# A decoder layer with attention and eight experts: sums of four steps in five quarters of batch two, and another passage from the attention loop to the experts, with a half-begun first expert

## The reference

```python
x = layernorm(x + linear_attention(x))             # 16 heads of 32, elu(q) + 1, elu(k) + 1
x = layernorm(x + cross_attention(x, ctx))         # 16 heads of 32, softmax over 2048 rows of context
x = layernorm(x + experts(x))

def experts(xf):                                   # 2048 tokens, 8 experts, two for each token
    probs = softmax(xf @ router_w + router_b)
    topk_p, topk_i = top_k(probs, 2)               # weights divided by their sum
    rank = place of the assignment among those of its expert, in order of the token
    keep = rank < 640                              # capacity: ceil(1.25 * 4096 / 8)
    h = gelu(buf[e] @ w1[e] + b1[e])               # 640 x 512 by 512 x 1024
    eo = h @ w2[e] + b2[e]                         # 640 x 1024 by 1024 x 512
    out[token] += eo[slot] * weight
```

## Time and profile before

| | us |
|---|---|
| median of 3 runs (1951.0 to 1957.52) | 1952.97 |
| the profiled execution's own time | 1955.99 |
| its span in the profile | 1954.2 |
| its mean granted PE clock | 0.982 of full speed |
| PE busy | 1886.4 (97%) |
| DVE busy | 1254.8 (64%) |
| ACT busy | 888.0 (45%) |
| POOL busy | 822.1 (42%) |

### The profile page before, as it was taken

One profiled execution on the slowest core, in us unless ns is written; L12 is line 12 of the kernel. 1 busy time (PEld: TensorE's weight loads), 2 busy tenths in 40 slices (PEclk: granted clock), 3 DMA queues, 4 the chain that ended last, 5 costly groups with the idle time before them and its releaser, 6 DMA issues.

```text
span 1954.2 us, 26706 instructions
## 1 busy us (share of the span) xinstructions
PE 1886.4 (97%) x10016; PEld 1281.6 (66%) x10016; DVE 1254.8 (64%) x2391; ACT 888.0 (45%) x1595; POOL 822.1 (42%) x740
## 2 busy tenths in 40 slices
PE   8999999989999999999999999999969999999996
PEld 6887677777655555555445545544439998899995
DVE  5675573257778788888678778777653444344457
ACT  3312322222566666666456456546724433344431
POOL 3002201100388788888567657665011223222132
PEclk9999999999999999999999999999978999999998
DMA  7003524573667476757434424421234444434453
GB/s 275 22 1 114 189 87 165 193 208 124 172 132 178 101 182 134 170 120 156 98 103 104 109 59 131 109 65 62 82 111 138 135 125 119 128 99 125 135 140 113
DMA packets 123777, 244.87 MB, mean 125 GB/s; under 512 B 11232, under 2 KB 29424, under 8 KB 119600
## 3 DMA queue, kind: packets, MB, share of 16 engines
q1 hardware_dynamic: 108608, 185.46, 32.0%
q0 software_dynamic: 13952, 55.61, 13.9%
q10 hardware_dynamic: 1088, 2.10, 0.3%
HBM read 148.46 MB, written 62.42 MB: 108 GB/s over the span
## 4 chain that ended last, share of the span: by engine, by line
PE 82%; DVE 13%; DMA 2%; issue 1%; ACT 1%; SPq 1%; POOL 1%; POOLq 0%; DVEq 0%; ACTq 0%
PE banks L1167 34%; PE banks L1440 12%; PE banks L1347 11%; PE banks L1317 10%; PE banks L1336 8%; DVE max L1638 8%; PE banks L1368 4%; PE banks L1173 2%; DMA k_parts<-out_lo 1%; DMA k_half<-in_xwk_t 0%; PE banks L1249 0%; DMA raw<-in_wk_t 0%; DVE stats_y L1869 0%; DVE den_c L1657 0%; POOL x_nat L2148 0%
## 5 line engine op out<-in xcount | busy, mean ns | idle before, releaser
L1638 DVE TENSOR_REDUCE max<-banks 128x1 f32<-128x512 f32 x1024 | 627.1, 680 | 144.3 <-PE banks L1317 143.4
L2137 POOL TENSOR_TENSOR probs<-probs,probs 128x512 f32<-128x512 f32 x464 | 583.0, 1291 | 249.0 <-PE banks L1347 249.0
L2017 ACT ACTIVATE probs<-banks 128x512 f32<-128x512 f32 x1024 | 520.2, 607 | 260.7 <-PE banks L1336 260.1
L1317 PE MATMUL banks<-k_stack,q_stack 98*128 98x512 f32 x1024 | 428.3, 425 | 4.0 <-DVE max L1638 2.7
L1336 PE MATMUL banks<-q_stack,k_stack 98*128 98x512 f32 x1024 | 377.1, 398 | 2.6 <-ACT probs L2017 2.6
L1317 PEld LDWEIGHTS banks<-k_stack,q_stack 98*128 98x128 f32 x1024 | 192.2, 188 | 194.5 <-DVE max L1638 106.2
L1347 PE MATMUL banks<-probs,v_grp 128*32 128x512 f32 x2048 | 251.7, 604 | 0.0
L1336 PEld LDWEIGHTS banks<-q_stack,k_stack 98*128 98x128 f32 x1024 | 191.7, 188 | 62.3 <-ACT probs L2017 17.8
L2184 POOL DMA_INDIRECT y_rows<-eo,tok x35 | 71.4, 2040 | 170.3 <-DVE eo L1839 116.1
L1826 DVE TENSOR_TENSOR hid_lo<-hid,hid_hi 128x640 fp32r<-128x640 f32 x64 | 52.8, 825 | 139.0 <-ACT hid_hi L2082 139.0
L1167 PE MATMUL banks<-w_hi,hid_hi 128*128 128x512 f32 x320 | 129.6, 405 | 2.3 <-DVE eo L1849 2.2
(11 more groups left out here) (263 smaller groups left out, 2806.7 us busy)
## 6 DMA issues: line engine op xcount, KB each, us to landing
k_stack<-k_parts SPq DMA_DIRECT2D x144, 256.0 KB, 5.3
w_raw<-in_L_ffn_w SPq DMA_DIRECT2D x16, 2048.0 KB, 8.4
probs<-probs POOLq DMA_DIRECT2D x31, 1024.0 KB, 10.1
q_stack<-q_parts SPq DMA_DIRECT2D x48, 256.0 KB
v_grp<-v_rows SPq DMA_DIRECT2D x48, 256.0 KB, 3.3
raw<-in_ctx_t SPq DMA_DIRECT2D x8, 1024.0 KB, 7.1
k_parts<-out_hi SPq DMA_DIRECT2D x32, 256.0 KB, 2.5
k_parts<-out_lo SPq DMA_DIRECT2D x32, 256.0 KB, 2.9
```

The lines of the kernel that those rows point to most:

```text
L1317: nc.tensor.matmul(out, queries_of(t)[:, j, tile_of(k)], keys_of(t)[0:STK + SHIFT, j, mc * HALF:(mc + 1) * HALF], start=True, stop=True) \
L1638: V.reduce_max(max4[:, tiles_of(t), :, :][:, k, j, mc:mc + 1], bank(bank_of["max", t, mc, k, j]), AX.X) \
L2017: S.activation(probs_of(t, s)[:, j, :], bank(bank_of["score", t, s, j]), ACT.Exp, scale=SCALE) \
L2137: G.tensor_tensor(a[:, j, :], a[:, j, :], b[:, j, :], ALU.add).then_inc(pair_added.sem, 1)
```

## The change

1. Five quarters of batch two, (turn, quarter) = (8,0), (8,1), (10,1), (13,0) and (13,1), go by fours as well: five `add_four` transfers more, five den units less. `pending` is kept sorted by due block, and a turn's den bank is begun by whichever unit comes first.
2. The third quarter of turn 7 has its den unit due one block sooner.
3. In the first three halves log_parts is no longer put into the bank by an identity product and copied back by ACT: DVE adds bank and log_parts.
4. A step WITH_PE beside one WITHOUT_PE is now taken only in turn 15.
5. In the last half y_nat goes into only two banks by an identity (tiles 0 and 1); DVE adds it to the banks of tiles 2 and 3, which now come first. log_parts goes in behind the rows.
6. In the last half's ranks the running sum comes from three more products with ones on PE, not from four small DVE operations. The copy that carries `before` on is left out there too.
7. `tokens` has two DVE operations for four.
8. The first 320 columns of the first expert's `up` f = 0 and f = 1 are multiplied by themselves (`up_first`), before and behind the last transposition (which touches only columns 512 to 639).

A few semaphores are shared or split otherwise. The core of the diff (semaphores, emptied banks and the engines' tables of stages left out):

```diff
+LAST_BEFORE_PLAIN = {(2 * NG - 1, 2)}
+
+LATER_FOURS = {(8, 0), (8, 1), (10, 1), (13, 0), (13, 1)}
...
+BY_VECTOR, BY_TENSOR = (2, 3), (0, 1)
...
-            return t * MT + s < B * NG * MT - FOUR
+            return t * MT + s < B * NG * MT - FOUR or (t, s // FOUR) in LATER_FOURS
...
-            begin_parts(b, h)
-            do("parts", b, h)
+            do("parts", b, h, ring=next_s_bank)
...
+            pending.sort(key=lambda due: due[0])
             while pending and pending[0][0] <= until:
                 _, t, s = pending.pop(0)
-                if s == (3 if by_fours(t, 0) else 1):
+                if t not in den_begun:
                     take_bank(("den", t), DEN)
+                    den_begun[t] = s
                 do("den", t, s)
                 if s == MT - 1:
                     do("copy_den", t)
-                    divisions.extend((t, q) for q in range(PIECES))
+                    tiles = BY_VECTOR + BY_TENSOR if t == LAST else range(HT)
+                    divisions.extend((t, k * SHARE + i) for k in tiles for i in range(SHARE))
                     divisions_from[0] = clock
...
-                if not busy or turn >= LAST - 2:
+                if not busy or turn == LAST:
...
-                        pending.append((clock + 4, turn, s + 1))
+                        pending.append((clock + (3 if (turn, s // FOUR) in LAST_BEFORE_PLAIN else 4), turn, s + 1))
...
         for k in range(HT):
             take_bank(("rows", b, h, k, LATE), next_s_bank.next())
+        for k in BY_TENSOR:
             do("rows_first", b, h, k)
-        begin_parts(b, h)
         loop_end = (scored, num_summed, den_summed, exp_done, num_copied, den_copied, pair_added, last_pair_added,
...
-        for k in range(HT):
+        for k in BY_VECTOR + BY_TENSOR:
             do("rows", b, h, k, LATE)
+        begin_parts(b, h)
...
+        for i in range(NS - 1):
             turn_xe(0, i)
             gather(1, i)
+        take_bank(("up", 0, 0), up_ring.next())
+        do("up_first", 0, 0)
+        turn_xe(0, NS - 1)
+        gather(1, NS - 1)
+        take_bank(("up", 0, 1), up_ring.next())
+        do("up_first", 0, 1)
...
+                    for k in range(HT - 1):
+                        accumulate(out[:, (k + 1) * E:HT * E],
+                                   [(ones[:, :], ms[:, k:k + 1, :].to_broadcast([P, HT - 1 - k, E]))], start=False,
+                                   stop=False)
+                    accumulate(out[:, 0:HT * E], [(ones[:, :], before[:, 0:1, :].to_broadcast([P, HT, E]))],
+                               start=False).then_inc(ranks_summed.sem, 1)
...
+                begun = e == 0 and f < 2
+                if not begun:
+                    free_bank("up", e, f)
...
+                up_products(e, f, (1,) if begun else (0, 1)).then_inc(up_summed.sem, 1)
...
+                    if k in BY_VECTOR:
+                        step.settle(V.tensor_tensor(row, got, row, ALU.add))
+                    done = V.bn_stats(stats4[:, k, :], row if k in BY_VECTOR else got)
...
+                    V.tensor_tensor(log_parts[:, :], bank(bank_of["parts", b, h]), log_parts[:, :], ALU.add) \
+                        .then_inc(parts_copied.sem, 1)
...
-                step.settle(V.tensor_tensor(tok_f[:, :], tok_f[:, :], table[:, 0, :], ALU.add))
-                step.settle(V.tensor_scalar(tok_f[:, :], tok_f[:, :], float(NTOK), None, ALU.add))
-                V.tensor_copy(tok[:, :], tok_f[:, :]).then_inc(tok_ready.sem, 1)
+                V.scalar_tensor_tensor(tok[:, :], tok_f[:, :], float(NTOK), table[:, 0, :], ALU.add, ALU.add) \
+                    .then_inc(tok_ready.sem, 1)
```

More of the change, by code:

```diff
@@ L518, in emptied @@
         def emptied(unit):
-            if unit[0] == "rows" and unit[-1] == LATE:
+            if unit[0] == "rows" and unit[-1] == LATE and unit[3] in BY_TENSOR:
                 return x2_done[unit[1:-1]]
@@ L1378, in rows @@
                 unit = ("rows", b, h, k, part)
-                out = bank(bank_of[unit]) if part == LATE else free_bank(*unit)
+                begun = part == LATE and k in BY_TENSOR
+                out = bank(bank_of[unit]) if begun else free_bank(*unit)
                 gs = {EARLY: range(NG - 1), LATE: (NG - 1,), WHOLE: range(NG)}[part]
@@ L1383, in rows @@
                 pe.wait_ge(*xwo_in[()])
-                accumulate(out, [(heads_t[:, g, tile_of(h * HT + k)], xwo[:, g, :]) for g in gs], start=part != LATE) \
+                accumulate(out, [(heads_t[:, g, tile_of(h * HT + k)], xwo[:, g, :]) for g in gs], start=not begun) \
                     .then_inc(xo_summed.sem, 1)
@@ L1392, in parts @@
             def parts(b, h):
+                last = (b, h) == (B - 1, NH - 1)
+                out = bank(bank_of["parts", b, h]) if last else free_bank("parts", b, h)
                 for g in range(NG):
-                    pe.wait_ge(*divided[turn_of[b * NG + g, h], HT - 1])
+                    pe.wait_ge(*divided[turn_of[b * NG + g, h], BY_TENSOR[-1] if last and g == NG - 1 else HT - 1])
                 pe.wait_ge(*folded[()])
-                by_column_groups(bank(bank_of["parts", b, h]),
-                                 [(head_w[:, g, :], heads_t[:, g, h * HALF:(h + 1) * HALF]) for g in range(NG)],
-                                 start=False).then_inc(parts_summed.sem, 1)
+                by_column_groups(out, [(head_w[:, g, :], heads_t[:, g, h * HALF:(h + 1) * HALF]) for g in range(NG)],
+                                 start=not last).then_inc(parts_summed.sem, 1)
             def logits(b, h):
@@ L1428, in turn_xe, with up_products, up_first @@
                 transpose_tile(out, xg[i]).then_inc(xe_turned.sem, 1)
+            def up_products(e, f, halves):
+                terms = [(w[:, c, tile_of(f)], x[:, c]) for c in range(NC)
+                         for w, x in ((w1_hi, xe_hi), (w1_hi, xe_lo), (w1_lo, xe_hi))]
+                both = pairs[bank_of["up", e, f] // 2]
+                for n, (w, x) in enumerate(terms):
+                    for h in halves:
+                        done = nc.tensor.matmul(both[:, h, 0:HC], w, x[:, h * HC:(h + 1) * HC],
+                                                start=n == 0, stop=n == len(terms) - 1)
+                return done
+            def up_first(e, f):
+                free_bank("up", e, f)
+                pe.wait_ge(*w1_split[e, NC - 1])
+                pe.wait_ge(*xe_split[e, HC // P])
+                up_products(e, f, (0,))
             def up(e, f):
-                first = bank_of["up", e, f] // 2
-                free_bank("up", e, f)
+                begun = e == 0 and f < 2
+                if not begun:
+                    free_bank("up", e, f)
                 if f == 0:
@@ L1435, in up @@
                     pe.wait_ge(*xe_split[e, NS - 1])
-                terms = [(w[:, c, tile_of(f)], x[:, c]) for c in range(NC)
-                         for w, x in ((w1_hi, xe_hi), (w1_hi, xe_lo), (w1_lo, xe_hi))]
-                for n, (w, x) in enumerate(terms):
-                    for h in range(2):
-                        done = nc.tensor.matmul(pairs[first][:, h, 0:HC], w, x[:, h * HC:(h + 1) * HC],
-                                                start=n == 0, stop=n == len(terms) - 1)
-                done.then_inc(up_summed.sem, 1)
+                up_products(e, f, (1,) if begun else (0, 1)).then_inc(up_summed.sem, 1)
             def finish(e, i):
@@ L2035, in x2 @@
                 late = ("rows", b, h, k, LATE)
-                S.activation(row, bank(bank_of[late]) if late in bank_of else row, ACT.Identity, bias=neg_shift[:, k:k + 1], scale=rs_y[:, k:k + 1]) \
+                S.activation(row, bank(bank_of[late]) if late in bank_of and k in BY_TENSOR else row, ACT.Identity, bias=neg_shift[:, k:k + 1], scale=rs_y[:, k:k + 1]) \
                     .then_inc(x2_done.sem, 1)
@@ L2043, in parts @@
             def parts(b, h):
-                act.wait_ge(*parts_summed[b, h])
-                S.activation(log_parts[:, :], bank(bank_of["parts", b, h]), ACT.Copy).then_inc(parts_copied.sem, 1)
+                if (b, h) == (B - 1, NH - 1):
+                    act.wait_ge(*parts_summed[b, h])
+                    S.activation(log_parts[:, :], bank(bank_of["parts", b, h]), ACT.Copy).then_inc(parts_copied.sem, 1)
             def route_exp(b, h):
```

44 lines of the change are left out of this document (29 added, 15 removed).

## The result

The changed kernel takes 1937.97 us (median of 4 runs, 1935.54 to 1940.76), the one before 1955.24 over its own 4 runs (1951.0 to 1959.72): a ratio of 0.9907 with a 95% interval of 0.9885 to 0.993. It is faster by 17.3 us; 15.7 was forecast, to 1937.5.

The account below looks back on a forecast made before the run. PE, busy 97% of the span, was taken as the bound. Terms 4.3 + 0.7 + 3.2 + 4.4 + 1.4 + 1.65 gave 15.7 us off the profiled 1955.99; median forecast 1937.5, range 1931 to 1946.

Parts of the forecast that it names:

- Den units: Loop, batch two: five den units less at 0.85 us of PE each, transfers hidden on POOL's queue; 4.3 us.
- Stall at 944: Loop, at 944.85: PE's wait for ACT's copy of turn 7's denominators goes; 0.7 us, bounds 0 and 0.7.
- Parts: First three halves: three identity products of 1.06 us leave PE, DVE's additions hide; 3.2 us, lower bound 1.1.
- Ranks' block: Block with ranks of (1, 0): 7.7 us rather than 12.13, saving 1.7 of wait and 2.7 of half clock; 4.4.
- Passage: From 1431.35 to 1475.7: statistics 1.6 sooner, ranks 0.7 late, tokens 0.5 sooner; 1.4 us, bounds 0 and 2.9.
- The ranks' step: Passage, last half: five products for two, starting 0.51 us apart at half clock, make DVE's read 0.7 us late.
- Half-begun expert: First expert: products around the last transposition hide its split and bring the clock back sooner; 1.65 us, bounds 0.5 and 2.2.
- 6.2 us behind 1466.8: First expert: without a wait the full clock can return at 1473.0 rather than 1475.7.
- The head: Stretch up to the mark in the loop's first turn; the prediction's sum has no term for it.
- B: Rival: the stall at 1346 moves, or only the profiled run had the dip; 11.3 us, 1941.7; chance 0.2.
- C: Rival: the passage brings nothing and the clock returns no sooner behind the transpositions; 13.1 us, 1939.9; chance 0.12.
- D: Rival: late transfers stop PE, 4.4 us each; all five 1959.3. Chance of one or two 0.1, all 0.03.

Follow-up runs that it names:

- e1: Changed kernel with the den units of the five batch-two quarters put back; the loop takes 902.89 us, 3.62 more.
- e6: Changed kernel with log_parts again added by identity product and copied back by ACT in the first three halves; loop 901.89 us, 2.6 more.
- e2: Changed kernel with a step WITH_PE beside one WITHOUT_PE taken in turns 13 to 15 again; loop 902.39 us, 3.1 more.
- e11: Changed kernel with a step WITH_PE beside one WITHOUT_PE taken in turns 13 and 15, not 14; loop 899.21 us, no idle time at the ranks.
- e10: Changed kernel plus 14 unread 128x128 filler products on PE behind the last half's logits; 1936.01 us, aggregate to f = 2 35.50 against 36.21.
- e3: Changed kernel with the five new quarters' den units due two blocks after the quarter's last step, not four; loop 899.19 us, nothing waits.
- e5: Changed kernel with all 36 four-step sums' den units due two blocks after the quarter's last step; loop 956.12 us, 56.9 more.
- e12: Changed kernel with fourteen batch-two quarters by fours rather than five; loop 918.69 us, 19.4 slower; whole 1958.25.

## Why the prediction was right, and where not

The sum was 15.7, and the profiled executions, whose own times are 1955.99 and 1937.93, differ by 18.1. Term by term:

- *Den units, 4.3:* 3.6 (e1). The step "5 x 0.85" took each block as PE's; three of the blocks had DVE close behind.
- *Stall at 944, 0.7:* the three blocks lose 1.76, of which 0.86 is one of the five units: 0.9. The wait didn't move elsewhere.
- *Parts, 3.2:* 3.14 in the three blocks, 2.6 in the loop (e6).
- *Ranks' block, 4.4:* 19.13 - 14.74 = 4.39 between the two profiles, but 2.8 in e2 with the same wait. The cause was right (e11), the size that of one execution: the 2.7 of half clock is as long as it happens to be. The four terms as forecast come to 12.6, as measured to 12.0; the loop lost 11.92.
- *Passage, 1.4:* 1.91 in the statistics (1.6 forecast), -0.25 in the ranks from the aggregate to rt_kp (-0.7), 0.49 in the tokens (0.5), 0.07 in the gathers: 2.2. The ranks' step was mis-sized in that the products of 24, 16 and 8 columns start 0.43 apart and not 0.51. The Trainium skill's rule that was weighed there ("TensorE: Matmul & The Clock Gate", "LDWEIGHTS (loading the stationary operand)") fails on e10: the same ten passes end 1.04 us sooner at full clock, so at half clock they do not take the 0.107 us of its formula.
- *Half-begun expert, 1.65:* 2.77 between the two profiles, 2.1 in the means. The step "6.2 us behind 1466.8" is the one that failed: the clock came back 2.9 us behind the first of the products (2.5 to 5.1 over the eleven executions), 5.8 us sooner than before and not 2.7, and in other executions of the same code 3.5. That it would come from the clock was right.
- *The head, 0:* 1.39, within what it varies by.

Both low terms and high ones were there, and the median's 17.3 contains the luck of both sets of runs. That 1937.5 was met to 0.5 us is luck in part: it was counted from a median of 1952.97, which a fourth run moved to 1955.24. Of the rivals, B falls by e11, C by the passage's 5.0, and D doesn't happen with five quarters (e3), though its mechanism is real (e5). What would have turned the change round was named only in passing ("DVE" under the step of the ranks) and stands in e12: more of the same edit loses all that it won, by a collision of small DVE operations with POOL that the trace of before shows only small: 1.22 and 0.90 us for two of them, at 1360.55 and 1362.05.

## What to carry to other kernels

Where one engine is busy 97% of the time, count what leaves it, block by block, and check in each block that the next engine isn't just behind; the sum held to within 1 us over a loop of 900. A wait costs more than itself by what the clock does afterwards (here 1.5 to 2.6 times), and that part varies between executions of the same code, so compare stretches over several profiles, not one. Ask the counts that another engine makes in this block for in the next one.

## What the runs showed of the hardware

- DVE operations of 0.2 us lasted up to 5.25 us beside four additions of POOL's (e12, three times), and PE stood still with them. While POOL stood still for 1.4 us, as in the changed kernel at 1019.05 to 1020.43, the same operation took 0.18. The Trainium skill, "GPSIMD Engine Reference", section "8. Key points", has the two engines share their SBUF interfaces, with contention for DVE instructions of certain kinds; the trace agrees that there is contention, with a size (up to 5 us for one operation) that the page doesn't give.
- It needs no transfer. The changed kernel has issued its last `add_four` at 1287.0, and yet three of the small operations around 1347 last until the POOL addition beside them ends, but each only for one of the four:

```profile
1344.62 5.00 POOL L2191 TENSOR_TENSOR probs<-probs,probs 128x512 f32<-128x512 f32 x4 [2.50 <-PE banks L1365]
...
1345.96 1.20 DVE L1810 TENSOR_TENSOR col_s<-weight 128x4 f32<-128x4 f32 x1
1347.19 1.22 DVE L1811 TENSOR_SCALAR col_s<-col_s 128x4 f32<-128x4 f32 x1
1348.44 0.18 DVE L1812 RECIPROCAL col_r<-col_s 128x4 f32<-128x4 f32 x1
1348.66 0.99 DVE L1813 TENSOR_TENSOR weight<-weight,col_r 128x8 f32<-128x8 f32 x1
```

  What makes one operation last over all four, as in e12, is open: there POOL had each time just issued a transfer, and its additions took 1.5 us each rather than 1.3. No run separates these.
- A RECIPROCAL beside the same additions kept its 0.18, and the maxima, which read PSUM, were not slowed either: 0.68 us each on the page before and 0.68 in e12.
- After a wait of the same 1.69 us ahead of the same products, the clock was at half for 3.4 us in one execution (e2) and 6.8 in the other (before). Behind the transpositions it came back at 8.0 to 10.8 us for the same code.
